# Attention on one core: the value product of the step two back moves from a step's end to the place in front of its fourth maximum and score

## The reference, cut to what matters

```
q = (x @ wq.T).reshape(B, S, 16, 8);  k, v: 4 heads of 8, each repeated 4 times
attn = einsum('bqhd,bkhd->bhqk', q, k) * scale
attn = where(causal, attn, -inf);  attn = softmax(attn)
out  = einsum('bhqk,bkhd->bqhd', attn, v) @ wo.T
```

## Time and profile before

| | |
|---|---|
| median of three runs | 1433.67 us (1433.6 to 1440.95) |
| span of the profiled execution | 1437.3 us |
| that execution's own time | not listed apart; its span alone is 3.6 us above the median |
| PE busy | 1150.2 us, 80% |
| DVE busy | 1108.8 us, 77% |
| ACT busy | 740.2 us, 51% |
| POOL busy | 677.0 us, 47% |

### The profile page before, as it was taken

How to read it: one execution, slowest core, us unless ns; L and a number is a source line. 1 busy time by engine, 2 the same in 40 slices (tenths; PEclk the granted TensorE clock), 3 DMA queues, 4 the chain that set the end, 5 groups by cost and what they waited for, 6 DMA issues and landing times. The chain is left out here.

```text
span 1437.3 us, 18717 instructions
## 1 busy us (share of the span) xinstructions
PE 1150.2 (80%) x5568; PEld 535.7 (37%) x5568; DVE 1108.8 (77%) x3046; ACT 740.2 (51%) x1619; POOL 677.0 (47%) x823
## 2 busy tenths in 40 slices
PE   3613896899998997775747677998999899989885
PEld 1201454555554554331412322343334333433232
DVE  5889555655788879689897697788998889888227
ACT  4644676137435444342321157575567556755772
POOL 7524584364777778657670022215331533153312
PEclk9855997999999998787877589999999999999998
DMA  4000101422111110003123120303020302000002
GB/s 115 0 0 1 49 2 26 142 75 69 54 37 44 44 40 6 0 1 65 24 48 55 39 47 1 66 1 55 1 38 1 55 1 38 1 4 1 4 1 59
DMA packets 33682, 47.02 MB, mean 33 GB/s; under 512 B 5023, under 2 KB 18207, under 8 KB 33279
## 3 DMA queue, kind: packets, MB, share of 16 engines
q1 hardware_dynamic: 30990, 43.84, 13.8%
q10 hardware_dynamic: 2592, 2.00, 0.5%
HBM read 39.14 MB, written 6.68 MB: 32 GB/s over the span
## 5 line engine op out<-in xcount | busy, mean ns | idle before, releaser
L1694 ACT ACTIVATE RB<-PS 128x512 f32<-128x512 f32 (+3 forms) x768 | 323.2, 502 | 183.3 <-PE PS L676 180.4
L624 PE MATMUL PS<-B 96*128 96x512 bf16 (+3 forms) x768 | 247.6, 349 | 44.2 <-DVE SS L1191 14.7
L676 PE MATMUL PS<-B 96*128 96x512 bf16 (+3 forms) x768 | 238.3, 333 | 24.2 <-ACT RB L1694 22.2
L1191 DVE CUSTOM_DVE_ANT_0 PS<-PS,w_msk 128x128 f32<-128x128 f32 (+3 forms) x512 | 242.4, 505 | 18.6 <-PE PS L624 18.1
L1964 POOL TENSOR_SCALAR_AFFINE_SELECT RB<-RB 128x512 f32<-128x512 f32 x128 | 81.0, 635 | 363.9 <-ACT RB L1694 363.9
L1194 DVE TENSOR_REDUCE SS<-PS 128x1 f32<-128x512 f32 x256 | 175.6, 686 | 32.9 <-PE PS L624 31.9
L693 PE MATMUL PS<-RB,B 128*32 128x512 f32 (+3 forms) x1536 | 169.0, 514 | 0.0
L624 PEld LDWEIGHTS PS<-B 96*128 96x128 bf16 x768 | 75.0, 99 | 228.8 <-DVE SS L1191 99.7
L1870 POOL TENSOR_TENSOR RB<-RB,B 128x512 f32<-128x512 f32 x64 | 82.2, 1286 | 89.3 <-DVE RB L1020 66.8
L676 PEld LDWEIGHTS PS<-B 96*128 96x128 bf16 x768 | 73.6, 98 | 105.7 <-ACT RB L1694 74.6
L1536 ACT ACTIVATE RB<-PS 128x512 f32<-128x512 f32 x72 | 42.8, 595 | 129.6 <-PE PS L438 129.5
(11 more groups left out here) (262 smaller groups left out, 2209.9 us busy)
## 6 DMA issues: line engine op xcount, KB each, us to landing
B<-scrW SPq DMA_DIRECT2D x128, 128.0 KB, 3.0
B<-scrQ SPq DMA_DIRECT2D x72, 128.0 KB
scrQ<-B SPq DMA_DIRECT2D x6, 384.0 KB, 3.7
B<-scrK SPq DMA_DIRECT2D x36, 64.0 KB
X<-in_x SPq DMA_DIRECT2D x8, 256.0 KB, 8.7
out_dram<-X SPq DMA_DIRECT2D x7, 256.0 KB, 3.2
B<-in_w SPq DMA_DIRECT2D x3, 576.0 KB, 4.9
B<-in_zeros SPq DMA_DIRECT2D x9, 128.0 KB
```

What stands on the lines that cost most here:

```text
L624: pe.matmul(p[:, 0:w], qs[u % 3][:, h, 128 * i:128 * i + 128], keys_of(u, h)[:, 512 * c:512 * c + w], start=True, stop=True).then_inc(s["m ...
L676: pe.matmul(p[:, 0:w], keys_of(u, 4 * kl + z)[:, 128 * kt:128 * kt + 128], qs[u % 3][:, 4 * kl + z, 512 * qc + off:512 * qc + 512], start= ...
L1191: ins = dve.tensor_tensor_reduce(p, p, msk[:, 512 - w:512], 1.0, LOWEST, ALU.add, ALU.max, MX[:, u % 2, i, h, c:c + 1])
L1694: act.activation(RB[:, 4 * (step % 3) + z, 0:w], bank(bank_of["score", step, z])[:, 0:w], ACT.Exp).then_inc(s["ex2"], 1)
```

## The change

`product_2(step - 2)` leaves the end of the step on PE and stands inside the loop over the four scores, at its fourth turn, ahead of M4 and S4. Nothing else is touched: no instruction is added or removed, and DVE, ACT, POOL and SP run the lists they ran. In the steps behind 191, which hold no scores, the product now stands ahead of the post slices and of `heads_2`.

```diff
                 for z in range(4):
+                    if z == 3 and 0 <= step - PLAG < 192:
+                        product_2(step - PLAG)
                     for v, n in ahead[z:z + 1]:
                         first_1(next_1(step), v, n)
                     if step < 192:
                         score_2(step, z)
...
                     if kt == 4 * GROUPS[n][2] + 3:
                         heads_2(n)
-                if 0 <= step - PLAG < 192:
-                    product_2(step - PLAG)
                 if u < 7 and r == 20:
                     guard_1(u + 1)
```

## The result

The changed kernel takes 1428.21 us (median of five runs, 1424.13 to 1431.41), and the kernel before 1437.13 in the same comparison (1433.6 to 1440.95). The medians are 8.9 us apart. The ratio as measured is 0.993, with a 95% interval of 0.9906 to 0.9955: about 10 us less. A second measurement, with five more runs, gave 1424.89 us and a ratio of 0.9918 (0.9901 to 0.9934). The forecast was 1421.5 us, a gain of 12.2, with a range of 1411 to 1433.

A forecast was written before the change was run, and what follows sets the result against it. PE was taken as the bound from 910 to 1335 us, DVE close behind. Terms 7.5 + 1.6 + 3 + 2.4 + 0.4 - 2.4 = 12.5 us, off 1433.67, gave 1421.2, stated as 1421.5, range 1411 to 1433.

The forecast's parts named there:

- (a): Main stretch: the expert product's 1.7 us wait takes a product of 1.07 us; 0.75 us kept per repeat.
- (d): Main stretch: a little wait before the fourth score's 1.51 us one is filled, 0.2 us per repeat.
- clock behind (c): Behind step 102's long wait: the drop to clock 0.50 loses 1.65 us in two repeats; half counted, 1.6 us.
- (c): Step 102 and its repeats: the fourth score's 1.51 us wait for ACT takes the product, 1.07 us each.
- steps 0 to 24: Stretch 821 to 910 us: five places with waits can take a product; 3 us gained, bounds 0 and 5.
- last stretch: From 1335 us: 0.8 us at step 166's wait, 1.6 in four post-slice steps, nothing in plain steps; 2.4 together.
- group ends: A group's first product now waits for ACT's copy of bank 7: 0.1 us lost at 24 ends, 2.4 us.
- step 25: The wait of 1.4 us for L1182 takes a narrow product, 0.4 us gained.
- (b): Step 94: the expert product's 1.03 us wait is filled, step 95's third maximum waits some 0.45; 0.5 us kept.
- rival (A): The wait only moves: PE arrives early and waits for DVE; gain 3.4 us, time 1430; chance 0.26.
- rival (B): Slower: at group ends the product waits for `sums`, delaying PE and DVE; time 1438 us; chance 0.09.
- Rival (C): More: waits are filled in full and the clock stays up; gain 22.3 us, time 1411; chance 0.13.

The follow-up runs named there:

- e10: The changed kernel with the product between the fourth maximum and the fourth score, not ahead of both: 1428.21 us, ratio 0.9935.
- e11: The kernel before, with the fourth maximum's matmul repeated eight times in steps 54, 102, 150 and four times in 62, 110, 158: 1433.07 us, ratio 0.9981.
- e4: The kernel before, with the fourth maximum's matmul of steps 54, 102 and 150 repeated eight times more: 1436.77 us, ratio 1.0.
- e3: The changed kernel, with the first product of each group (32 of 192) back at the step's end: 1433.93 us, ratio 0.9997.
- e7: The changed kernel, with the product of steps 0 to 23 kept at the step's end: 1426.41 us, ratio 0.9934.
- e8b: The kernel before, with the new place only in steps 164 to 191 without a post slice or heads' turn on PE: 1437.96 us, ratio 0.9995.
- e2: The kernel before, with the product in its new place in steps 24 to 163 only: 1428.94 us, ratio 0.9957.

## Why the prediction was right, and where its terms were not

The time came out 6.7 us above the forecast in the first measurement and 3.4 in the second, inside the range, and the gain by the first ratio is 10.0 us against 12.2. Of the 6.7 us, 3.5 are the base: the gain was taken off 1433.67, the median of three, in the belief that the profiled execution was a slow one. Its span of 1437.3 was an ordinary one, as 27 other executions of that kernel show (median 1437.14). The main mechanism, a ready product put ahead of waits, holds. But the sum came near by terms that missed on both sides:

| term | forecast | measured |
|---|---|---|
| (a) to (d), three repeats | 7.5 | 2.6 |
| clock behind (c) | 1.6 | 3.2 |
| steps 0 to 24 | 3 | -0.8 |
| last stretch | 2.4 | 5.3, of it 1.2 clock |
| group ends | -2.4 | -0.2 in steps 120 to 140 alone |
| step 25, and the rest of 24 to 164 | 0.4 | 2.6, not taken apart (0.2 in step 25) |
| step 164, and behind step 191 | 0 | -1.0 |
| ahead of step 0, by chance | 0 | -1.3 |
| sum | 12.5 | 10.4, as by the spans |

*Waits (a) to (d).* (a) and (c) were filled as forecast and mostly given back; (b) was not filled. PE in steps 94 and 95:

```profile
1118.32 0.27 PE L676 MATMUL PS<-B 96*128 96x256 bf16 x1
1119.45 1.96 PE L739 MATMUL PS<-WW,B 128*128 128x512 f32 x4 [0.86 <-DVE SS L1194]
...
1122.37 0.34 PE L624 MATMUL PS<-B 96*128 96x384 bf16 x1 [0.68 <-DVE HN L1367]
```

L739 still waits 0.86 us of its 1.03, since PE comes to it early, and M3 of step 95 waits 0.68 for L1367, where the forecast had 0.45. What stays is 0.47 us, by luck near the forecast's 0.5: 0.96 won in step 93, whose S4 had waited 0.78, less 0.49 here. The forecast had not listed that wait; the earlier trace rows has six waits of L676 for ACT, three of 1.5 us and these three. (c) gives 1.08 at step 102 and loses 0.95 at 103, net 0.1 against 1.07: the step that failed was "With the product ahead of S4 that is 1.07 us", which did not ask what the product had covered in its old place. (a) gives 0.87, and up to the guard of step 116 0.62 are gone again, where L665 waits 1.15 us and waited 0.69 before: net 0.25 against 0.75. That (a) causes the guard's wait is argued; e10, with M4 ahead of the product, takes 0.4 us less in that step. Together some 0.85 a repeat. This is rival (A), which had 0.7. The mark "new waits for DVE's L1367 of more than 0.5 us each time" was met in half of the six (0.68 us in step 95 and its repeats, 0.38 in step 111 and its), and L739's waits fell to 4.2 us and not below 3.

*The clock.* Both falls behind step 102 and 150 are gone, so 3.2 us and not half of it; the term that was too small is "I count half". e11 gives the same 1.62 a repeat with the product unmoved. The 1.6 to 1.65 us, worked out from the earlier trace rows, was right in size. Why the falls are gone is shown in part only. e4 shows that filling the one wait would not have done, and e11 that filling both did. But e3 left the 1.51 us wait as it was and kept the clock behind it in steps 102 and 150, and lost it in step 54. The Trainium skill, "TensorE: Matmul & The Clock Gate", section "HAM oscillation", has idle gaps between bursts drop the clock; the gaps of its own case, waits for DMAs, are longer than the 1.5 us here. The traces agree in that falls stand behind waits, differ in that 1.5 us was enough, and add that what follows does not hang on the wait just ahead alone.

*The first stretch* was forecast at 3 with 0 as the lower end; it lost 0.8 (1.1 in the second profile), outside its bounds. Most of what changed there goes with clock falls that came and went. Step 2 takes 2.68 us in place of 4.41: a fall of 3.4 us there is gone. Steps 16 to 18 take 12.97 in place of 10.29. The changed kernel's clock from step 17 on, and that of the kernel before in its step 17:

```profile
881.90:888.70 6.80, 6.80 (x27) 1.98 (x30) 5.62 (x18) 4.46 (x8) 3.63 (x7) 0.50 0.01 1
```

```profile
882.07:884.56 2.49, 2.38 (x18) 0.79 (x17) 2.49 (x12) 2.05 (x4) 2.08 (x7) 1.00 0.00 0
```

All five traces with the product ahead of a score or maximum in step 17 have this fall, none of the eight with it at the step's end. Before, PE waited 1.52 us at the end of step 16 and then had the product of 0.64 us to do; now it waits 1.30 and 0.30 and has done the product already. With it goes a delay on ACT, which does the late preparation between exponentials. ACT in step 18:

```profile
889.97 0.60 ACT L1694 ACTIVATE RB<-PS 128x512 f32<-128x512 f32 x1 [1.17 <-PE PS L676]
```

It waits 1.17 us for S4, which stands behind a product that takes 1.35 us at the lower clock, and the preparation's L1625, behind that exponential, starts 4.43 us after the step's first score and not 2.39. The forecast looked at the waits alone and had neither the clock nor this delay. How much of the loss each of them makes is not shown; that the place costs something there, e7 shows.

*The last stretch* gave 5.3 us, more than twice its term. Two steps failed. "I give such steps nothing": e8b has 1.8 us from plain steps. The argument held for a ring of equal pieces: in steps 180 and 181, all of full width, the wait moved to S3 as forecast and nothing was won (5.02 and 5.13 us). But the block of keys on the diagonal makes narrow scores beside wide ones. The place of steps 184 and 185 after, and before:

```profile
1371.25 0.99 PE L676 MATMUL PS<-B 96*128 96x128 bf16 x4
1372.17 0.64 PE L693 MATMUL PS<-RB,B 128*32 128x256 f32 x8
1372.74 1.50 PE L676 MATMUL PS<-B 96*128 96x512 bf16 x4
```

```profile
1381.65 0.82 PE L676 MATMUL PS<-B 96*128 96x512 bf16 x3
1382.73 0.39 PE L676 MATMUL PS<-B 96*128 96x512 bf16 x1 [0.26 <-ACT RB L1694]
1383.05 0.64 PE L693 MATMUL PS<-RB,B 128*32 128x256 f32 x8
```

With the product between two steps' scores the four wide ones run through, where S4 had waited 0.26 us. Of the 24 waits of a score in the earlier trace rows nine are left. ACT's idle time from step 164 to 191 fell from 15.9 to 9.9 us. And the clock fall at 1344.7 us is gone, 1.2 us that the forecast had not counted at all. Of the terms it did have, the post slices came true (0.38 us in step 182, forecast 0.4), and the 1.5 us wait of step 166 did not: that step gained 0.12 us, and the one before it 0.42, against 0.8.

*Group ends.* The walk through step 126 was right: a wait of 0.28 us by its numbers, and 0.29 in the trace, and the step takes 2.99 us in place of 2.89, the 0.1 of the forecast.

```profile
1214.42 0.28 PE L676 MATMUL PS<-B 96*128 96x256 bf16 x1
1215.00 1.07 PE L693 MATMUL PS<-RB,B 128*32 128x512 f32 x8 [0.29 <-ACT RB L1701]
```

But such waits came 9 times for 2.4 us and not at 24 ends, and steps 120 to 140, with four of them, lost 0.2 us in all. With the other products ahead, the new place is the better one there: in e3, without it, steps 120 to 142 take 0.85 us more. This removes rival (B), and "2 to 8 us" of waits for L1701 holds. The cut's waits are hidden under the matmuls but for 0.4 us, where the forecast had none. Rival (C) fails by the first stretch and by what was given back, though its clock term in the main stretch was the right one.

## What to carry to other kernels

When a ready instruction is moved ahead of a wait, ask first what it covered where it stood: behind a turn that another engine must answer, it was the cover, and taking it away brings a new wait a step later (0.95 of 1.08 us here). Where the clock falls behind long waits, look at all of the long waits and not at the one before the fall: filling the first of two was worth nothing, filling both 1.6 us, and one and the same wait of 1.5 us was followed by a fall in one repeat and not in another. And price a place in a ring with the sizes that really pass it, narrow and wide, since equal pieces turn for nothing and unequal ones don't. Last, a move that is worth something in one stretch can bring a clock fall in another: look at the clock by step in every stretch before a loss is put down to an engine.

## What the runs showed of the hardware

**A clock fall can be handed on.** In e4 a wait filled at step 102 moved the fall of 3.4 us to the 1.72 us wait of step 110, in both repeats that had one.

**A new wait can bring a new fall, in some executions.** The guard's wait at step 68 grew from 0.69 to 1.15 us with the change. In e2 and e3 the clock fell behind it (1046.7 and 1051.1 us), and step 69 took 4.22 and 3.83 us in place of 2.67; in the changed kernel's two profiles and in e7 it did not.

**A short DVE operation beside a POOL one.** Four more matmuls at step 110 won 0.47 us that no theory had. Kernel before, DVE and POOL:

```profile
1170.25 1.11 DVE L924 TENSOR_TENSOR SC<-SC 128x32 f32<-128x32 f32 x3
...
1170.69 0.63 POOL L1964 TENSOR_SCALAR_AFFINE_SELECT RB<-RB 128x512 f32<-128x512 f32 x1 [1.29 <-ACT RB L1694]
```

and e11_filled_both:

```profile
1164.71 0.64 DVE L927 TENSOR_TENSOR SC<-SC 128x32 f32<-128x32 f32 x3
...
1165.99 0.63 POOL L1967 TENSOR_SCALAR_AFFINE_SELECT RB<-RB 128x512 f32<-128x512 f32 x1 [2.14 <-ACT RB L1697]
```

Three operations in SBUF take 0.64 us alone. With POOL's cut starting inside them they take 1.11: the third ran 0.66 us in place of 0.19. A maximum (L1191) that reads PSUM kept its 0.60 us beside the same cut. The Trainium skill, "SBUF — State Buffer", section "Terms", says that these two engines share a pair of ports and the loser is held up entirely; the rows agree. The changed kernel has the short form there too, so by this 0.47 of (a)'s 0.87 us is the short form and not the filled wait. That the overlap causes the lengthening rests on these rows alone: no run moved the cut and nothing else.
